# Adjacency in 64x64x64 products, weighted sums set by set in fp32, opening and last step in another order

## The chip, the cores and the metric

The kernel runs on one core of a Trainium2 chip. The metric is the device time of the whole program in microseconds (us), lower is better.

## The reference, cut to what matters

`x` is 128 sets of 64 nodes with 256 features, `adj` a 64x64 matrix of zeros and ones that all sets share.

```python
h = relu(layernorm(x))
q, k, v = h @ Wq.T, h @ Wk.T, h @ Wv.T
rel = adj.T * (q @ k.T)                       # per set, 64 x 64
rel = rel / norm(rel, axis=2)
x = x + rel @ v
h = relu(layernorm(x))
for _ in range(3):                            # gated graph steps
    a = adj @ h                               # in_mat and out_mat are both adj
    av = concat([a, a])
    z = sigmoid(av @ W3.T + b3 + h @ U3.T + bu3)
    r = sigmoid(av @ W4.T + b4 + h @ U3.T + bu3)
    hv = tanh(av @ W5.T + b5 + (r * h) @ U5.T + bu5)
    h = (1 - z) * h + z * hv
out = x + h
```

All of it is fp32. Nothing joins one set with another.

## The kernel before, in words

The 8192 tokens (set and node) are cut into 16 groups of 512 tokens, that is of four pairs of sets: 128 tokens (two sets) fill the 128 partitions, `Q = 4` such pairs stand side by side (`q`). The 256 features are two halves of 128 (`c`, or `o` for outputs). Features stand on the partitions in most products, so that a gate's output is a 128x512 tile in one PSUM bank.

Large products are made in three parts (`product`, L408): each fp32 operand is split into a rounded part `_hi` and a rest `_lo` of type fp32r, and hi*hi, hi*lo and lo*hi are added in PSUM. ScalarE (ACT) makes `_hi` (L724), VectorE (DVE) subtracts to get `_lo` (L921). Small products are plain fp32: the scores (`scores_by_set`, L497), the turns through the identity, and the adjacency product (`adjacency`, L564). A plain fp32 matmul leaves two records in the profile, a fp32r one leaves one.

**Windows.** Two groups, X and Y, run through the three gated steps in turn. One step of one group is a window `w = 6i + k`; even `k` is one group, odd `k` the other. On TensorE (PE) a window is: reset gate from the state (`reset_gate_h`, 12 products into `gate`), reset gate from the adjacency result (`reset_gate_a`, 12), candidate from `a` (12 into `cand`), update gate (12), candidate from `r*h` (12), and then the adjacency product for the next window of the other group into `fea`. That one takes the other group's state as tokens by features (`t_s`, or `h0` at a group's first step) as the stationary operand and multiplies `adjT` with it. `adjT` is 128x128 with `adj.T` twice on its diagonal and zeros elsewhere; so one 128x128x128 product serves two sets, with half of its work on zeros, and a window has 8 of them (4 pairs, 2 feature halves).

Meanwhile DVE updates the other group's state, turns it in blocks of 32, SyncE (SP) sends it to DRAM and back (`turn_state`) to finish the turn, and ACT copies it into `t_s` (`take_back`). After the adjacency product ACT rounds `fea` into `a_hi` and DVE subtracts `a_lo` (`split_a`), which free `fea`.

**Attention beside it.** In the 7 rounds of the loop (6 windows each) windows `k = 2` and `k = 4` also make queries, values and scores of the next groups: `values` writes `tok`, ACT and DVE split it into `v_hi` and `v_lo`; scores go to `fea`, DVE masks them into `S`, ACT rounds `S_hi` and squares `sq`, DVE makes `S_lo`. At the start of windows 3 and 5 `weighted_sum` makes rel @ v from them with 12 fp32r matmuls of 128x128x256. The normalised input `hx` of a group is turned through DRAM as well (`turn_hx`: one store of 512 KB, then four loads).

**Opening and end.** The first two groups pass through an opening that is written out instruction by instruction (weights are split there too, and the product M of Wq and Wk is made in one piece). The last window's state (`new_half`, `transpose_state`) is turned by PE, added to the residual and stored in one piece.

Order is fixed by the code: each engine works its own queue off in program order and waits on semaphores for the others.

## Time and profile before

| | |
|---|---|
| median of 3 runs | 908.33 us (907.57 to 908.65) |
| the profiled execution | 907.36 us, of which 905.6 us is the span of the trace |
| PE busy | 891.7 us, 98% |
| DVE busy | 756.7 us, 84% |
| ACT busy | 520.9 us, 58% |
| granted clock | 0.995 of full over the span |

The time outside the span (1.8 us) is start and end of the program. Busy time of PE is the union of its records; records of successive matmuls overlap, so the distance from one start to the next, and not the length of a record, tells what one costs.

### The profile page before, as it was taken

Reading aid. Unit: us, or ns where it says so; the run is one execution under the profiler, and the core shown is the slowest. Engines: PE = TensorE matmul, PEld = TensorE weight load, DVE = VectorE, ACT = ScalarE, POOL = GpSimd, SP = SyncE. Lnnn points to the kernel's source line nnn. Section 1 sums busy time; section 2 is a strip of 40 time slices with the busy share of each in tenths; the row PEclk is TensorE's granted clock in tenths of the full one; section 3 lists DMA queues with packets and bytes.
Section 4 is the critical chain, followed back from the end, with each engine's and each line's share of the span. In section 5 each row is a group of like instructions: output and inputs, shape, how many; then the busy total and the mean of one; then the engine's idle time right before and its main releaser. Section 6 shows DMA issues by size and latency. Waiting matters only on the chain.

```text
span 905.6 us, 15070 instructions
## 1 busy us (share of the span) xinstructions
PE 891.7 (98%) x4984; PEld 763.0 (84%) x4984; DVE 756.7 (84%) x1527; ACT 520.9 (58%) x892; POOL 111.0 (12%) x161
## 2 busy tenths in 40 slices
PE   8999999999999999999999999999999999999996
PEld 7878888888888888888888888888888888888885
DVE  6888879888799888988988888988879888798665
ACT  5465664656456564665645656556664656555552
POOL 2110102101021010210101101120101101020000
PEclk9999999999999999999999999999999999999998
DMA  6023222623235142441414513154221622233212
GB/s 182 6 69 114 93 94 99 203 69 113 90 123 184 46 142 89 140 167 42 150 58 141 184 69 116 46 176 148 93 93 70 203 98 93 93 116 117 87 54 93
DMA packets 75394, 98.73 MB, mean 109 GB/s; under 512 B 8176, under 2 KB 65776, under 8 KB 75376
## 3 DMA queue, kind: packets, MB, share of 16 engines
q1 hardware_dynamic: 75376, 98.50, 33.0%
q8 instruction: 10, 0.16, 0.1%
q14 instruction: 8, 0.07, 0.0%
HBM read 50.76 MB, written 47.71 MB: 109 GB/s over the span
## 4 chain that ended last, share of the span: by engine, by line
PE 95%; DVE 2%; issue 1%; DMA 1%; ACT 1%; SPq 0%; DVEq 0%
PE gate L410 14%; PE gate L411 14%; PE gate L412 14%; PE cand L410 10%; PE cand L412 9%; PE cand L411 9%; PE fea L564 9%; PE tok L410 3%; PE tok L411 2%; PE tok L412 2%; PE fea L497 2%; PE fea L411 1%; PE fea L410 1%; PE fea L412 1%; DMA x_s<-x 1%
## 5 line engine op out<-in xcount | busy, mean ns | idle before, releaser
L808 ACT ACTIVATE r_s<-gate,b_r 128x512 f32<-128x512 f32 x96 | 65.7, 690 | 123.8 <-PE gate L412 123.8
L1129 DVE TENSOR_TENSOR rh<-r_s,h 128x512 f32<-128x512 f32 x96 | 69.8, 760 | 29.5 <-ACT r_s L808 28.9
L821 ACT ACTIVATE z_s<-gate,b_z 128x512 f32<-128x512 f32 x96 | 64.1, 683 | 48.0 <-PE gate L412 48.0
L827 ACT ACTIVATE c_s<-cand,b_c 128x512 f32<-128x512 f32 x96 | 64.4, 686 | 26.2 <-PE cand L412 25.5
L724 ACT ACTIVATE h_hi<-h 128x512 fp32r<-128x512 f32 x92 | 56.8, 628 | 38.1 <-DVE h L921 22.4
L355 POOL TENSOR_TENSOR rstd<-vare,minus_half 128x4 f32<-128x4 f32 x32 | 42.0, 1312 | 297.3 <-DVE vare L955 297.3
L410 PE MATMUL gate<-h_hi,W_hi_u 128*128 128x512 f32 x192 | 77.9, 406 | 0.2 <-DVE h_lo L921 0.2
L1101 DVE SCALAR_TENSOR_TENSOR d_s<-z_s,h 128x512 f32<-128x512 f32 x96 | 63.5, 685 | 17.5 <-ACT z_s L821 17.5
L410 PE MATMUL cand<-rh_hi,W_hi_u 128*128 128x512 f32 x192 | 76.5, 398 | 0.0
L410 PE MATMUL gate<-a_hi,W_hi_w 128*128 128x512 f32 x192 | 75.0, 390 | 1.1 <-DVE a_lo L921 1.1
L411 PE MATMUL gate<-h_lo,W_hi_u 128*128 128x512 f32 x192 | 75.1, 391 | 0.0
L412 PE MATMUL gate<-h_hi,W_lo_u 128*128 128x512 f32 x192 | 74.8, 390 | 0.0
L412 PE MATMUL cand<-rh_hi,W_lo_u 128*128 128x512 f32 x192 | 74.8, 390 | 0.0
L412 PE MATMUL gate<-a_hi,W_lo_w 128*128 128x512 f32 x192 | 74.8, 390 | 0.0
L411 PE MATMUL gate<-a_lo,W_hi_w 128*128 128x512 f32 x192 | 74.8, 390 | 0.0
L411 PE MATMUL cand<-rh_lo,W_hi_u 128*128 128x512 f32 x192 | 74.8, 389 | 0.0
L412 PE MATMUL gate<-a_hi,W_lo_wz 128*128 128x512 f32 x192 | 74.7, 389 | 0.0
L410 PE MATMUL gate<-a_hi,W_hi_wz 128*128 128x512 f32 x192 | 74.7, 389 | 0.0
L411 PE MATMUL gate<-a_lo,W_hi_wz 128*128 128x512 f32 x192 | 74.7, 389 | 0.0
L410 PE MATMUL cand<-a_hi,W_hi_w 128*128 128x512 f32 x192 | 74.7, 389 | 0.0
L411 PE MATMUL cand<-a_lo,W_hi_w 128*128 128x512 f32 x192 | 74.7, 389 | 0.0
L412 PE MATMUL cand<-a_hi,W_lo_w 128*128 128x512 f32 x192 | 74.7, 389 | 0.0
(150 smaller groups left out, 2202.7 us busy)
## 6 DMA issues: line engine op xcount, KB each, us to landing
h_back<-h_trip SPq DMA_DIRECT2D x216, 128.0 KB, 2.8
h_trip<-h_turned SPq DMA_DIRECT2D x40, 512.0 KB, 2.6
out<-o_s SPq DMA_DIRECT2D x16, 512.0 KB, 3.8
x_s<-x SPq DMA_DIRECT2D x15, 512.0 KB, 4.9
hx_trip<-hx SPq DMA_DIRECT2D x14, 512.0 KB, 3.5
hx_back<-hx_trip SPq DMA_DIRECT2D x56, 128.0 KB, 2.8
h_trip<-h_blk SPq DMA_DIRECT2D x14, 512.0 KB, 3.0
h_trip_last<-h_turned SPq DMA_DIRECT2D x7, 512.0 KB, 3.5
```

The costliest lines, as they stand in the source:

```text
L355: nc.gpsimd.tensor_tensor(rstd[n][:], vare[n][:], minus_half[:], ALU.pow).then_inc(rstd_ready[n], 1)
L410: nc.tensor.matmul(dst, l_hi, r_hi, start=start, stop=False, skip_group_check=True)
L411: nc.tensor.matmul(dst, l_hi, r_lo, start=False, stop=False, skip_group_check=True)
L412: return nc.tensor.matmul(dst, l_lo, r_hi, start=False, stop=stop, skip_group_check=True)
L497: last = nc.tensor.matmul(feaS[half(e), q, half(e)], hxT[:, c, nodes], q_s[:, c, nodes], start=c == 0, stop=c == C - 1)
L564: last = nc.tensor.matmul(fea[:, c, graph_pair(q)], src[:, q, c * P:(c + 1) * P], adjT[:], start=True, stop=True)
L724: return nc.scalar.activation(dst, src, ACT.Copy)
L808: nc.scalar.activation(r_s[:, c, :], gate[:, c, :], ACT.Sigmoid, bias=b_r[:, c:c + 1]).then_inc(r_ready, 1)
L821: nc.scalar.activation(z_s[:, c, :], gate[:, c, :], ACT.Sigmoid, bias=b_z[:, c:c + 1]).then_inc(z_ready, 1)
L827: nc.scalar.activation(c_s[:, c, :], cand[:, c, :], ACT.Tanh, bias=b_c[:, c:c + 1]).then_inc(c_ready, 1)
L1101: nc.vector.scalar_tensor_tensor(d_s[:, c, :], z_s[:, c, :], 1.0, h[s][:, c, :], ALU.subtract, ALU.mult).then_inc(diff_ready, 1)
L1129: nc.vector.tensor_tensor(rh[:, c, :], r_s[:, c, :], h[s][:, c, :], ALU.mult).then_inc(rh_ready, 1)
```

## The change: what it does

1. **Adjacency.** The 8 fp32 products of 128x128x128 of a window become 32 of 64x64x64, one for each set, feature half and half of that (`f`). Each uses a quarter of the array: rows by set (`e`), columns by `f`; the results of set 0 of every pair go to one PSUM bank, those of set 1 to the other. Both banks are now reported full at the end. `split_a` goes by bank (set) in place of feature half, and `reset_gate_a` first makes its 8 matmuls with `a_hi`, then waits for both `a_lo` and makes 4.
2. **Weighted sum** in the loop: 8 fp32 matmuls of 64x64x256 from plain `S` and `v_s` in place of the 12 in fp32r. `v_s` is a plain copy by DVE, so ACT's `v_hi` and `S_hi` and DVE's `S_lo` are gone in the loop. To spread the row halves, two of the four pairs have their sets swapped: `turn_hx` stores in three transfers in place of one, and `square_S` is four instructions of ACT in place of two.
3. A semaphore add on PE (`sources_seen`) that carries the wait stands ahead of these small products, so that none of them is started before its source is there.
4. **Loop.** The two reset gate steps of window 1 stand at the end of the loop body of the round before, not at the start of their own.
5. **Opening**: M is made and split in two halves, group 1's turn goes ahead of the norms of group 0, splits and copies are put in another order on DVE and ACT, norms of group 1 use `fea`. The plain copies of `h` come behind the splits.
6. **Last step** by halves of 256 tokens: candidate, tanh, update, turn and store.

```diff
+        def key_half(q, e):
+            return half(e if q < HQ else 1 - e)
+        def set_columns(t, e):
+            return t[:].rearrange("p c (q e n) -> p c q e n", q=Q, e=2)[:, :, :, e, :]
+        def set_bank(e):
+            return fea[:, e, :].rearrange("p (c q n) -> p c q n", c=C, q=Q)
...
             def turn_hx(g, s):
                 sp.wait_ge(hx_ready, Q * (g + 1))
-                sp.dma_start(hx_trip[s], hx[:].rearrange("p q d -> p (q d)")).then_inc(hx_out, 16)
-                sp.wait_ge(hx_out, 16 * (g - 1))
+                trip, hx_r = rows_by_set(hx_trip[s]), rows_by_set(hx[:].rearrange("p q d -> p (q d)"))
+                sp.dma_start(trip[:, :, 0, :], hx_r[:, :, 0, :]).then_inc(hx_out, 16)
+                for e in range(2):
+                    sp.dma_start(trip[half(1 - e), :, 1, :], hx_r[half(e), :, 1, :]).then_inc(hx_out, 16)
+                sp.wait_ge(hx_out, 48 * (g - 1))
                 blocks_back(hx_back, hx_trip[s], hx_in)
...
-            def weighted_sum(g, n_tok, n_v):
-                pe.wait_ge(S_hi_ready, g + 1)
-                pe.wait_ge(S_lo_ready, g + 1)
-                pe.wait_ge(v_hi_ready, 2 * g + 2)
+            def weighted_sum(n_v, n_rel):
                 tok_done(n_v)
-                for b in range(2):
-                    tok_wait(n_tok, b)
-                    for q in range(HQ * b, HQ * b + HQ):
-                        last = product(tok[:, q, :], (S_hi[:, q, :], S_lo[:, q, :]),
-                                       (v_hi[:, q, :], v_lo[:, q, :]), True, True)
-                    last.then_inc(tok_full, 1)
+                pe.wait_ge(fea_taken, 2 * n_rel + 2)
+                pe.sem_inc(sources_seen, 1)
+                for j in range(HQ):
+                    for q in (j, j + HQ):
+                        for e in range(2):
+                            keys = key_half(q, e)
+                            last = nc.tensor.matmul(tok[half(e), q, :], S[keys, q, keys], v_s[keys, q, :],
+                                                    start=True, stop=True)
+                last.then_inc(tok_full, 2)
...
-            def adjacency(c, src, n):
-                fea_wait(n, c)
-                for q in range(Q):
-                    last = nc.tensor.matmul(fea[:, c, graph_pair(q)], src[:, q, c * P:(c + 1) * P], adjT[:],
-                                            start=True, stop=True)
-                last.then_inc(fea_full, 1)
+            def adjacency(src, n, t_full=None):
+                fea_wait(n, 1)
+                for c in range(C):
+                    if t_full is not None:
+                        pe.wait_ge(t_ready, t_full + c)
+                    if c == 0 or t_full is not None:
+                        pe.sem_inc(sources_seen, 1)
+                    for q in range(Q):
+                        for f in range(2):
+                            part = slice(c * P + f * N, c * P + (f + 1) * N)
+                            for e in range(2):
+                                last = nc.tensor.matmul(set_bank(e)[half(f), c, q, :], src[half(e), q, part],
+                                                        adjT[half(e), half(e)], start=True, stop=True)
+                last.then_inc(fea_full, 2)
...
             def reset_gate_a(w, s, n_a):
-                for c in range(C):
-                    pe.wait_ge(a_hi_ready, 2 * w + (c + 1))
-                    pe.wait_ge(fea_taken, 2 * n_a + (c + 1))
-                    for o in range(C):
-                        last = product(gate[:, o, :], weight("w4", c, o), (a_hi[s][:, c, :], a_lo[s][:, c, :]),
-                                       False, c == C - 1)
-                        if c == C - 1:
-                            last.then_inc(r_full, 1)
+                pe.wait_ge(a_hi_ready, 2 * w + 2)
+                for o in range(C):
+                    for c in range(C):
+                        w_hi, w_lo = weight("w4", c, o)
+                        one(gate[:, o, :], w_hi, a_hi[s][:, c, :])
+                        one(gate[:, o, :], w_lo, a_hi[s][:, c, :])
+                pe.wait_ge(fea_taken, 2 * n_a + 2)
+                for o in range(C):
+                    for c in range(C):
+                        last = one(gate[:, o, :], weight("w4", c, o)[0], a_lo[s][:, c, :], stop=c == C - 1)
+                    last.then_inc(r_full, 1)
...
+            def candidate_rh_last():
+                pe.wait_ge(rh_hi_ready, 2 * LAST)
+                pe.wait_ge(rh_lo_ready, 2 * LAST)
+                for e in range(2):
+                    for o in range(C):
+                        if e == 1:
+                            pe.wait_ge(c_ready, 2 * LAST - 1 + o)
+                        for c in range(C):
+                            last = product(cand[:, o, tokens(e)], weight("u5", c, o),
+                                           (rh_hi[:, c, tokens(e)], rh_lo[:, c, tokens(e)]), False, c == C - 1)
+                        last.then_inc(c_full, 1)
...
             values(0, n("v 0"), (1,))
+            transpose_hx(1, cand, turned_full)
             norms_start(0, n("norm 0"))
-            transpose_hx(1, cand, turned_full)
...
-            def split_a(s, c, n):
-                fea_wait(n, c)
-                copy(a_hi[s][:, c, :], fea[:, c, :]).then_inc(a_hi_ready, 1)
+            def split_a(s, e, n):
+                fea_wait(n, e)
+                copy(set_columns(a_hi[s], e), set_bank(e)).then_inc(a_hi_ready, 1)
...
                 if attention and k == 2:
-                    split_v(use("v X"))
-                    round_S(use("rel X"))
                     square_S(use("rel X"))
...
-            split_weight(3, "w4", sum4)
+            split_weight(3, "u3", raw["u3"])
+            split_weight(4, "w4", sum4)
+            split_S(0)
             take_norm_start(n("norm 0"))
-            split_S(0)
...
-            take_norm(1)
             split_S(1)
-            split_weight(4, "w5", sum5)
+            split_weight(5, "w5", sum5)
+            take_norm_start(n("norm 1"))
+            copy_new_start(0, cand)
...
-            new_half(6 * PAIRS, 1, 0)
-            new_half(6 * PAIRS, 1, 1)
+            for e in range(2):
+                for c in range(C):
+                    new_last(e, c)
             add_resid(G - 1, 1, use_in_end("final 0"), PAIRS - 1)
```

How the rows stand on PE at the end of window 2, where the adjacency product and the weighted sum meet, before (`t_s` the turned state, `v_hi`/`v_lo` and `S_hi`/`S_lo` the split values and scores):

```order
L412 MATMUL cand<-rh_hi,W_lo_u 128x512
L666 REGISTER_ALU
L435 ISA [waits t_ready]
L564 MATMUL fea<-adjT,t_s 128x128 [waits fea_taken]
L564 MATMUL fea<-adjT,t_s 128x128 x3
L666 REGISTER_ALU
L564 MATMUL fea<-adjT,t_s 128x128 [waits fea_taken,t_ready]
L564 MATMUL fea<-adjT,t_s 128x128 x3
L538 REGISTER_ALU
L430 REGISTER_ALU [waits v_hi_ready,S_lo_ready,S_hi_ready]
```

The same place of PE in the changed kernel (`S` and `v_s` are the plain scores and values):

```order
L436 MATMUL cand<-rh_hi,W_lo_u 128x512
L462 ISA
L587 REGISTER_ALU [waits fea_taken]
L594 MATMUL fea<-adjT,t_s 64x64 [waits t_ready]
L594 MATMUL fea<-adjT,t_s 64x64 x15
L587 REGISTER_ALU
L594 MATMUL fea<-adjT,t_s 64x64 [waits t_ready]
L594 MATMUL fea<-adjT,t_s 64x64 x15
L457 REGISTER_ALU
L562 REGISTER_ALU [waits tok_taken]
L568 MATMUL tok<-v_s,S 64x256 [waits fea_taken]
L568 MATMUL tok<-v_s,S 64x256 x7
```

Eight products became 32, and the twelve matmuls of the weighted sum behind them became eight that use quarters of the array too; the waits for `S_hi`, `S_lo` and `v_hi` are gone.

On DVE the end of the attention's work in window 2 (`v` the values in `tok`, `S` the masked scores, `sq` their squares), before:

```order
L921 TENSOR_TENSOR v_lo<-tok,v_hi 128x512
L927 ISA
L1000 TENSOR_TENSOR S<-fea,mask 64x4x64 x2
L921 TENSOR_TENSOR S_lo<-S,S_hi 128x512
L1025 STREAM_TRANSPOSE sq_turned<-sq 128x256
L1028 TENSOR_REDUCE sq_part<-sq_turned 128x8
```

And in the changed kernel:

```order
L1072 COPY v_s<-tok 128x512
L1002 ISA
L1081 TENSOR_TENSOR S<-fea,mask 64x4x64 x2
L1106 STREAM_TRANSPOSE sq_turned<-sq 128x256
L1109 TENSOR_REDUCE sq_part<-sq_turned 128x8
```

`S_lo` is gone from DVE's row, and the subtraction that made `v_lo` is a copy that waits for PE alone.

## Rows read from the trace of the kernel before

**Rows 1.** The page, part 1: busy us (share of the span) and instructions.
```profile
PE 891.7 (98%) x4984; PEld 763.0 (84%) x4984; DVE 756.7 (84%) x1527; ACT 520.9 (58%) x892; POOL 111.0 (12%) x161
```
**Rows 2.** Stretches from adjacency to adjacency: us; PE, PEld, DVE, ACT, POOL busy; PEclk.
```profile
164.92:180.32 15.40, 15.40 (x77) 13.05 (x76) 13.45 (x30) 10.37 (x18) 2.73 (x3) 1.00 0.53 179
180.32:202.62 22.30, 22.30 (x145) 19.25 (x144) 18.90 (x38) 11.74 (x22) 1.01 (x1) 1.00 0.22 73
...
241.78:258.63 16.85, 16.85 (x90) 14.49 (x89) 16.31 (x40) 7.92 (x13) 2.43 (x2) 1.00 0.18 62
...
sum 109.11, PE 109.11 PEld 93.50 DVE 94.25 ACT 64.15 POOL 14.19; mean PE 18.18 PEld 15.58 DVE 15.71 ACT 10.69 POOL 2.36
```
**Rows 3.** Waits of PE: who for whom, us in total, times, longest.
```profile
PE tok L557 <- DVE h L921: 2.7, 1, 2.7
PE tok L410 <- issue: 2.1, 2, 1.5
PE gate L410 <- DVE a_lo L921: 1.1, 1, 1.1
```
**Rows 4.** Groups of PE by shape: adjacency and scores; busy us, mean ns.
```profile
L564 PE MATMUL fea<-adjT,t_s 128*128 128x128 f32 x512 | 62.2, 275 | 0.0
L564 PE MATMUL fea<-adjT,h 128*128 128x128 f32 x256 | 31.2, 275 | 0.1
L497 PE MATMUL fea<-q_s,hxT 128*64 128x64 f32 x448 | 16.1, 225 | 0.0
```
**Rows 5.** Timeline of PE, an adjacency product: start, length, what.
```profile
865.94 1.95 PE L564 MATMUL fea<-adjT,t_s 128*128 128x128 f32 x16
867.64 0.48 PE L410 MATMUL gate<-h_hi,W_hi_u 128*128 128x512 f32 x1
867.95 0.40 PE L411 MATMUL gate<-h_lo,W_hi_u 128*128 128x512 f32 x1
```
**Rows 6.** Timeline of PE, one group's scores and their neighbours.
```profile
128.52 0.28 PE L412 MATMUL tok<-W_hi_v,hxT_lo 128*128 128x256 f32 x1
128.73 1.15 PE L497 MATMUL fea<-q_s,hxT 128*64 128x64 f32 x32
130.15 0.39 PE L411 MATMUL cand<-rh_lo,W_hi_u 128*128 128x512 f32 x1
```
**Rows 7.** Timeline of PE cut at 128.745 (scores) and at 865.98 (adjacency).
```profile
128.73 0.28 PE L497 MATMUL fea<-q_s,hxT 128*64 128x64 f32 x2
...
865.94 0.27 PE L564 MATMUL fea<-adjT,t_s 128*128 128x128 f32 x1
```
**Rows 8.** Timeline of PE in the opening: the product M, 128x256 in fp32.
```profile
7.40 1.89 PE L676 MATMUL gate<-d_s 128*128 128x256 f32 x8
```
**Rows 9.** Timelines of ACT and DVE: last `a_hi` and `a_lo` of window 1's adjacency.
```profile
182.30 0.60 ACT L724 ACTIVATE a_hi<-fea 128x512 fp32r<-128x512 f32 x1 [0.30 <-PE fea L564]
...
185.09 0.65 DVE L921 TENSOR_TENSOR a_lo<-fea,a_hi 128x512 fp32r<-128x512 f32 x1
```
**Rows 10.** Timelines of SP and DVE: the turn of group X's `hx`.
```profile
177.62 0.34 SPq L242 DMA_DIRECT2D hx_trip<-hx  x1
181.38 1.75 SPq L237 DMA_DIRECT2D hx_back<-hx_trip  x4
...
185.67 1.28 DVE L969 STREAM_TRANSPOSE hxT<-hx_back 128x512 f32<-128x512 f32 x2
```
**Rows 11.** Timelines of PE and DVE in the opening.
```profile
41.06 0.36 PE L410 MATMUL tok<-v_hi,S_hi 128*128 128x256 f32 x1 [1.53 <-issue]
...
40.27 0.69 DVE L921 TENSOR_TENSOR S_lo<-S,S_hi 128x512 fp32r<-128x512 f32 x1
```
**Rows 12.** Timelines of DVE and SP at the end.
```profile
895.55 1.29 DVE L1092 TENSOR_TENSOR o_s<-h_back,resid 128x512 f32<-128x512 f32 x2
898.80 0.69 DVE L921 TENSOR_TENSOR h<-c_s,d_s 128x512 f32<-128x512 f32 x1
...
902.17 0.40 SPq L338 DMA_DIRECT2D out<-o_s  x1
```

230 lines of the change are left out of this document (140 added, 90 removed).

## The prediction, made before the changed kernel had run

> **What bounds the kernel now.** I read the page's busy times first. PE is busy for 98% of the span, the next engine, DVE, for 84% [rows 1]. An average can hide a stage with another limit, so the stretches of a round come next: window by window, from one adjacency product to the next, PE is busy for exactly as long as the stretch lasts, and the sum over a round's six windows is 109.11 us of 109.11 [rows 2]. The table of PE's waits has only single waits, all in the opening and at the end [rows 3]. So in the loop each microsecond taken from PE's row is a microsecond of the kernel, as long as the others keep up, and each one added is lost. DVE is the one to watch: 94.25 us in a round of 109.11, and 16.31 of 16.85 in window 5 [rows 2].
>
> A record's length says little on PE, because records overlap; I use distances between starts.
>
> **The adjacency product.** A window's product is 16 records (8 matmuls, two records each) and there are 512 + 256 records [rows 4], so 48 windows have one. It begins at 865.94; the two records behind it start at 867.64 and 867.95, and a fp32r matmul of 512 columns takes 0.227 us: a window without attention has 60 of them and this product in 15.40 us [rows 2], (15.40 - 1.78) / 60. So it ends at 867.95 - 0.23 = 867.72 and costs 1.78 us, 0.112 per record of 128 columns [rows 5]. Half of its multiplications are with the zeros of `adjT`.
>
> The new one has 64 records of 64 columns, each on a quarter of the array. No row shows quarters; the nearest is the scores: 32 records of 64 columns, each on half of the array's columns. The values in front end at 128.52 + 0.12 = 128.64 (0.12 for 256 columns, below), the candidate behind starts its second matmul at 130.15, so the scores take until 129.92: 1.28 us with getting in and out [rows 6]. Their 1.15 us less the 0.22 of a last record's own length leave 0.93, 0.058 for two records. How do two records fit into 0.058, when one of 128 columns takes 0.112? Cut at 128.745 the timeline has two records of the scores, started within 15 ns, while on the whole array only one is there 40 ns after the start [rows 7]. So two products on different column halves run side by side, and the hardware even takes the second half's product past the second record of the first (the records of one product must follow each other, as on the whole array). I take it that row halves do the same: four records for each 0.058 us, 16 such steps, and so the time of the scores, 1.28 us. That saves 1.78 - 1.28 = 0.50 us in each of 48 windows: **24.0 us**. Bounds from the nearest rows: nothing better than four at a time with no price for entry and exit, 0.93 us, -40.8 us in all; and, with one product for each 0.058 us, 32 steps and the same 0.35 us of entry and exit, 2.21 us, +20.6 us in all. I take the value in between, because the scores' row is the nearest in shape and kind and its price for a change of mode is in it.
>
> Here the Trainium skill speaks against the change: "PSUM — Partial Sum Buffer", section on engine and sequencer instructions, says that matmuls start and complete in program order. By that rule the second record of a product holds up the next product on another quarter; the scores' rate would come out the same (one product a step), and the adjacency would take the 2.21 us. The two starts within 15 ns [rows 7] do not look like that order, since the first product's own second record can't be one of them. It stays a rival.
>
> **The weighted sum.** Windows that begin with it last 16.85 us, those without anything extra 15.40 [rows 2]: 1.45 us for 12 matmuls of 256 columns, 0.12 each. It becomes 16 records of 256 columns on quarters, directly behind the adjacency, so with no other change of mode. A record of 256 columns in fp32 on the whole array takes (1.89 - 0.38) / 7 = 0.216 us, 0.38 being the last one's length [rows 8]. Four steps of it are 0.87 us. 14 x (1.45 - 0.87) = **8.1 us**. The bound from above, one product a step and a step for the last one's second record, is 9 x 0.216 = 1.94 us, +6.9 us in all. From below 0.87 stands: a quarter can't take its columns faster than the whole array does. I take 0.87, with the adjacency's reading.
>
> **What the other engines do meanwhile.** The loop's windows become 0.5 us shorter, those with a weighted sum 1.1. Is anybody late then?
> - `a_hi` used to be rounded for the first feature half while the second was still multiplied; now both banks come at the end. Last `a_hi` ended 182.90, counted from the product's start at 180.32 2.6 us [rows 2, 9]. Now the banks are there at 1.3 + 0.2, two rounds of 0.6 follow: 2.8. `reset_gate_a` starts at 1.28 + 12 x 0.227 = 4.0. Cover: 1.2 us; cost none.
> - `a_lo` ended at 185.74, 5.4 us after the product's start [rows 9], in an order of DVE that stays. It is now wanted at 4.0 + 8 x 0.227 = 5.8. Cover 0.4 us, none lost; in the opening's last window, where PE waited 1.1 us for it [rows 3], the new order gives that back.
> - DVE in window 5 had 16.31 us of work, 0.7 of it `S_lo`, which goes; the window becomes 15.8. It can run behind by 0 to 0.3 us and catch up in the next, which has 2 us to spare. Over a round DVE has 94.25 - 1.4 = 92.9 us to do in 109.1 - 4.1 = 105.0. Cost none; if it were not caught up, 7 x 0.3 = 2 us.
> - `turn_hx` issues three stores at 0.34 us each where there was one, in pieces of half a KB; issue to the loads' issue was 3.8 us, and the loads' end falls about where DVE turns it, at 185.67 [rows 10]. I expect it 1 to 2 us later. Queued behind it on DVE is `rh` of window 2, which then is late too; but the candidate that wants it has queries, values and scores before it, 6.9 us (22.30 - 15.40 [rows 2]). Cost none. SP's next state transfer is behind these stores by under 1 us, with the same cover.
> - The waits moved onto semaphore adds stand on PE's sequencer; before it lie 12 matmuls, 2.7 us, with waits long over. `tok` by a plain copy costs DVE what the subtraction did. Moving `reset_gate` of window 1 past the loop's end changes no instruction, and no wait of PE stands there now [rows 3]. Cost none.
>
> **Opening.** PE waits 1.5 us before the second weighted sum at 41.06 [rows 3, 11]; its DVE row is `S_lo` at 40.27 [rows 11], behind the norms that wait for PE. In the new order `S_lo` comes before the norms, and the two copies of `h` (2 x 0.6) are moved behind it. I count 1.5 us. The wait for `a_lo` is 1.1. The halves of M, and the turn that now fills the wait for the squares, I put at 0.9 us together, within 0 (something else is late then) and 2. Sum **3.5 us**, 1 to 5.
>
> **End.** The candidate by halves costs 24 matmuls of 256 columns where there were 12 of 512: 24 x 0.12 - 12 x 0.227 = +0.16 us. DVE is the limit: it finishes the other group's output until 896.84, then 4 operations until 899.49 [rows 12]; now it has 8 of about 0.4, until 900.0. Then half of the turn, half of the addition: the last store is issued at about 901.7 in place of 902.17 [rows 12] and is half as large. **0.8 us**, from 2 gained to 0.5 lost.
>
> **Sum** against the profiled execution's own 907.36 us (905.6 span, 1.8 around it): 24.0 + 8.1 + 3.5 + 0.8 = 36.4, so 871.0. The median stands 1.0 above that execution: **872 us**. Own range 865 to 881, from 0.1 us of entry and exit more or less per window (5 us), opening and end.
>
> **Rivals.**
> 1. *Products in order (slower).* One step a product: +20.6 and +6.9, less 4.3 of opening and end: +23.2, 931 us. It decides when two records of one product cannot be passed by another quarter's; it turns the sign once a window's product takes over 1.78 us. For it: the rate of the scores alone, which both readings explain. Against it: the two starts [rows 7].
> 2. *PE can't start records faster (slower, or nearly the same).* The closest starts on average are 0.93 / 32 = 29 ns [rows 6]. If that is the issue and not the columns, 64 records take 1.86 + 0.35 = 2.21 us (+20.6), while the weighted sum's long records still gain 8.1: +20.6 - 8.1 - 4.3 = +8.2, 916 us. Against it: two starts within 15 ns. The Trainium skill ("TensorE: Matmul & The Clock Gate", section "Wait — 56ns, not 53.3ns?") gives a floor of about 25 ns between two starts, however few the columns; no row here shows it, and by it 64 records would take 1.6 us and the whole come to an estimated 904.
> 3. *A new wait.* Shorter windows meet a chain that doesn't shrink: state turned, stored, loaded, `t_s`; or the late `hx`. At 0.3 us in each of 48 windows, 14.4 us of the gain are lost: 886 us; at worst all of the loop's 32.1, and 904 is left. For it: DVE's 16.31 of 16.85; against it: the covers above.
>
> **Chances.** Forecast 0.70; rival 1 0.10; rival 2 0.06; rival 3 0.14. The range reaches from the forecast's lower end to the worst of rival 3: 864 to 906, with under 0.2 outside, most of it rivals 1 and 2. Under 0.2% (1.8 us) this kernel's measurement tells nothing. Faster: the forecast and rival 3 less 0.01, 0.83; slower: rivals 1 and 2 less 0.01, 0.15; those two hundredths are the chance of the same.
>
> **What would show it.** In the new profile 64 records of an adjacency product within 1.15 us, the window without attention at 14.9 us from product to product and the one with a weighted sum at 15.8, four starts within some 30 ns, then a gap of 58; ACT's and DVE's waits for PE shorter, no wait of PE for `a_hi`, `a_lo` or `t_s`. If the records come in twos, the window lasts 15.8 and rival 1 or 2 holds (1: the weighted sum takes 1.9 us too; 2: it takes 0.9). If the product takes 1.3 us and the window is still over 15.1, PE has a new wait with a name, and rival 3 holds. I am wrong in the main point if quarters don't run four at a time.

## The result and the profile after

The changed kernel takes 917.69 us (median of 4 runs, 916.27 to 919.55) where the kernel before takes 908.33: a ratio of 1.0099, 95% interval 1.0086 to 1.0112. It is slower by 1%; the forecast was 872 us. The profiled execution took 917.08 us, 915.3 of them in the trace.

From the page of the changed kernel: part 1 (busy us, share, instructions), the granted clock in 40 slices, and the queue that brings instructions (pieces, MB, share).

```profile
PE 881.5 (96%) x7356; PEld 718.7 (79%) x7356; DVE 750.6 (82%) x1518; ACT 493.4 (54%) x881; POOL 122.3 (13%) x161
...
PEclk9999999899998999989999899999999999999998
...
q8 instruction: 72, 1.18, 0.5%
```

The last two lines on the page of the kernel before:

```profile
PEclk9999999999999999999999999999999999999998
...
q8 instruction: 10, 0.16, 0.1%
```

PE's share fell from 98% [rows 1] to 96%, some slices in the middle show less than the full clock, and 1.18 MB of instructions were fetched where 0.16 were. Now the round window by window, as in [rows 2] (us; PE, PEld, DVE, ACT, POOL busy; PEclk, DMA share, GB/s):

```profile
160.41:181.83 21.42, 18.00 (x126) 14.04 (x125) 14.00 (x31) 10.49 (x19) 2.72 (x3) 0.84 0.51 162
181.83:203.65 21.82, 21.82 (x194) 18.41 (x193) 18.17 (x38) 10.56 (x20) 1.01 (x1) 1.00 0.14 50
203.65:219.57 15.92, 15.92 (x142) 12.79 (x141) 14.20 (x36) 10.44 (x19) 1.80 (x2) 1.00 0.39 118
219.57:241.91 22.34, 22.11 (x194) 18.33 (x193) 17.56 (x30) 12.52 (x24) 3.05 (x6) 1.00 0.32 106
241.91:257.80 15.89, 15.89 (x141) 12.78 (x141) 15.38 (x37) 7.32 (x13) 2.43 (x2) 1.00 0.20 67
257.80:272.81 15.01, 15.01 (x126) 12.14 (x125) 13.72 (x22) 8.90 (x16) 4.98 (x7) 1.00 0.63 197
sum 112.40, PE 108.75 PEld 88.49 DVE 93.03 ACT 60.23 POOL 16.00; mean PE 18.12 PEld 14.75 DVE 15.51 ACT 10.04 POOL 2.67
```

Four windows are shorter, as forecast or nearly, and the fourth row's is as long as before (22.34). The first row, the answer to 15.40 us [rows 2], lasts 21.42. It is the one in which PE's loop jumps back. There are six such windows: 21.42, 21.48, 21.70, 21.67, 19.98 and 20.34 us. PE's waits name the same place six times, and the second row is new too (who for whom, us in total, times, longest); before there was one wait for `a_lo`, in the opening [rows 3]:

```profile
PE cand L434 <- issue: 19.8, 6, 3.4
PE gate L439 <- DVE a_lo L996: 2.5, 8, 0.9
```

"Issue" says that PE waited for no other engine: nothing was handed to it by its sequencer, the unit that reads PE's instructions in order, takes the waits and the jumps, and hands the products on. PE's timeline there (start, length, what, idle time ahead):

```profile
165.94 0.39 PE L439 MATMUL gate<-a_hi,W_lo_w 128*128 128x512 f32 x1
166.17 1.09 PE L439 MATMUL gate<-a_lo,W_hi_w 128*128 128x512 f32 x4
170.69 0.79 PE L434 MATMUL cand<-a_hi,W_hi_w 128*128 128x512 f32 x1 [3.42 <-issue]
171.28 0.63 PE L435 MATMUL cand<-a_lo,W_hi_w 128*128 128x512 f32 x1
171.70 0.63 PE L436 MATMUL cand<-a_hi,W_lo_w 128*128 128x512 f32 x1
172.13 0.63 PE L434 MATMUL cand<-a_hi,W_hi_w 128*128 128x512 f32 x1
```

The last products of the body end at 167.26, the first of the next pass starts 3.42 us later, and from there starts are 0.427 us apart instead of 0.227: the granted clock is at the lower of its two levels, 1.2 in place of 2.4 GHz. The trace's records of the jumps and of the stretches at the lower clock say it for all six (us):

```
                          before            changed kernel
jump taken, six times     0.234 0.213 0.208 4.33  4.08  4.17  4.31  4.04  4.33
                          0.208 0.207 0.208
lower clock in the loop   none              6.8   6.8   6.8   6.8   3.4   3.4
```

The six windows are 36.6 us longer than six of 15.0. PE idles for 19.8 us of that. Of the 34.0 us at the lower clock 3.5 lie in the idle time (in the first window it falls at 169.73, before the product at 170.69), and half of the other 30.6, 15.3 us, is lost by products at half the rate. That leaves 1.5 us. About 1.0 of it is that the idle time is counted from the end of the last record, 0.16 us behind the place where the next product would have started (0.39 - 0.227).

The product itself did what was forecast (PE's timeline, the whole product, and the same cut at 181.845):

```profile
181.83 1.16 PE L594 MATMUL fea<-adjT,t_s 64*64 64x64 f32 x64
182.92 0.50 PE L434 MATMUL gate<-h_hi,W_hi_u 128*128 128x512 f32 x1
...
181.83 0.28 PE L594 MATMUL fea<-adjT,t_s 64*64 64x64 f32 x3
```

64 records in 1.16 us, three of them begun within 15 ns [rows 7 for before]. In PE's compiled code the two matmuls of a product stand one behind the other, both on the same quarter of the array. The plain window fell from 15.40 to 14.92 us behind the loop.

### The profile page after: what moved, and what is told of

It is laid out like the page before. It is cut to its first block, busy times and chain, and to the rows that moved or that the text cites. A ratio compares the mean times of both kernels' runs of the same rounds, so it can differ in the third digit from the quotient of the medians.

```text
span 915.3 us, 19786 instructions
## 1 busy us (share of the span) xinstructions
PE 881.5 (96%) x7356; PEld 718.7 (79%) x7356; DVE 750.6 (82%) x1518; ACT 493.4 (54%) x881; POOL 122.3 (13%) x161
## 3 DMA queue, kind: packets, MB, share of 16 engines
q8 instruction: 72, 1.18, 0.5%
## 4 chain that ended last, share of the span: by engine, by line
PE 69%; issue 14%; DVE 10%; ACT 3%; POOL 3%; DMA 1%; DVEq 0%; SPq 0%; POOLq 0%; ACTq 0%
PE gate L439 10%; PE cand L434 8%; PE gate L434 8%; PE cand L435 7%; PE cand L436 7%; PE gate L435 7%; PE gate L436 7%; PE fea L594 4%; DVE c_s L1190 2%; PE fea L524 2%; POOL rstd L379 2%; PE tok L434 2%; PE tok L435 1%; PE tok L436 1%; PE fea L434 1%
## 5 line engine op out<-in xcount | busy, mean ns | idle before, releaser
L870 ACT ACTIVATE r_s<-gate,b_r 128x512 f32<-128x512 f32 x96 | 60.8, 685 | 106.0 <-PE gate L439 106.0
L434 PE MATMUL cand<-a_hi,W_hi_w 128*128 128x512 f32 x192 | 80.5, 419 | 19.8 <-issue 19.8
L1222 DVE TENSOR_TENSOR rh<-r_s,h 128x512 f32<-128x512 f32 x96 | 66.4, 732 | 18.7 <-ACT r_s L870 17.5
L434 PE MATMUL gate<-h_hi,W_hi_u 128*128 128x512 f32 x192 | 80.3, 418 | 0.3 <-DVE h_lo L996 0.3
L436 PE MATMUL cand<-a_hi,W_lo_w 128*128 128x512 f32 x192 | 79.8, 416 | 0.0
L435 PE MATMUL cand<-a_lo,W_hi_w 128*128 128x512 f32 x192 | 79.8, 415 | 0.0
L776 ACT ACTIVATE rh_hi<-rh 128x512 fp32r<-128x512 f32 x96 | 58.2, 631 | 38.8 <-DVE rh L1222 38.8
L434 PE MATMUL cand<-rh_hi,W_hi_u 128*128 128x512 f32 (+1 forms) x196 | 77.3, 394 | 0.0
L436 PE MATMUL cand<-rh_hi,W_lo_u 128*128 128x512 f32 (+1 forms) x196 | 75.5, 385 | 0.0
L435 PE MATMUL cand<-rh_lo,W_hi_u 128*128 128x512 f32 (+1 forms) x196 | 75.4, 385 | 0.0
```

Source lines behind the costliest of these rows:

```text
L434: nc.tensor.matmul(dst, l_hi, r_hi, start=start, stop=False, skip_group_check=True)
L435: nc.tensor.matmul(dst, l_hi, r_lo, start=False, stop=False, skip_group_check=True)
L436: return nc.tensor.matmul(dst, l_lo, r_hi, start=False, stop=stop, skip_group_check=True)
L776: return nc.scalar.activation(dst, src, ACT.Copy)
L870: nc.scalar.activation(r_s[:, c, :], gate[:, c, :], ACT.Sigmoid, bias=b_r[:, c:c + 1]).then_inc(r_ready, 1)
L1222: nc.vector.tensor_tensor(rh[:, c, :], r_s[:, c, :], h[s][:, c, :], ALU.mult).then_inc(rh_ready, 1)
```

## The experiments

I held three theories on the long windows. **A:** the loop body of PE has grown from 1316 to 1908 instructions (each small product is a weight load and a matmul, twice in fp32), and is too long to be still at hand when the loop jumps back. **B:** the step moved to the body's end, or the small products themselves, make the wait. **C:** the clock falls because the small products are too light. Theory **E** came with the first run: part of what is missing besides is PE waiting for the second `a_lo`. All runs are compared with runs of the kernel before made beside them on the same chip (908.4 to 909.6 us). The counts of instructions are those of PE's compiled code, numbered from its beginning. The instruction queue's row counts pieces: 1.18 MB in 72 are 16 KB each, which is 256 instructions (2732 instructions of the kernel before are 10.7 such pieces, and 10 were fetched).

### 1 and 2. No jump

```diff
-            with pe.Fori(0, PAIRS - 1) as i:
+            for i in range(PAIRS - 1):
```

On PE alone, in the changed kernel and in the kernel before. The loop has seven rounds and so six jumps back; the expectations' "six times" are these jumps.

> TensorE's loop of the changed kernel is written out six times and every other engine keeps its loop, so TensorE's work and every wait are the same and only the jump back at the end of a round is gone. Theory A (the changed loop body of 1908 TensorE instructions is too long to be still at hand when the jump goes back to its first one; the jump took 4.33 us, the instruction queue moved 1.18 MB against 0.16, and the windows that begin with the jump took 21.42, 21.48, 21.70, 21.67, 19.98 and 20.34 us against 15.0 for their like): these windows fall to 15.0, 36.9 us go, 878 to 881 us. Theory B (the window is long because of the work moved to the body's end and the products' order, not because of the jump): the time stays at 912 to 919. Theory C (a clock that falls because the small products are too light): no change at the window, and half clock there as before.

> The same edit in the kernel before: TensorE's loop written out six times. Theory A: its body of 1316 instructions is still at hand at the jump (0.234 us for the jump in the trace), so nothing is to be had: 906 to 909 us. If writing the loop out helps every such kernel (a rival to A: the jump always costs), it falls by more than 3 us. If straight code is fetched too slowly to keep up, it is longer.

Measured: changed kernel 883.9 us, ratio 0.9716 (0.9700 to 0.9732); kernel before 909.4, ratio 1.0003 (0.9993 to 1.0014). So the jump costs the changed kernel 34 us and the kernel before nothing. Theory B would have left the order and the products in place, and with them the loss; it is out, and so is "a loop always costs". Theory C is out too: with the same small products the loop of this run has no stretch at the lower clock. 883.9 is 3 to 6 above what I expected, and 12 above the forecast. Windows of the changed kernel without its jump, and PE's wait for `a_lo` over the whole execution:

```profile
161.14:176.28 15.14, 15.14 (x126) 12.09 (x125) 13.79 (x30) 9.70 (x19) 2.72 (x3) 1.00 0.53 171
176.28:198.56 22.28, 22.12 (x194) 18.33 (x193) 18.29 (x38) 11.10 (x22) 1.01 (x1) 1.00 0.29 93
198.56:214.34 15.78, 15.78 (x142) 12.63 (x141) 14.06 (x36) 10.45 (x19) 1.67 (x2) 1.00 0.39 119
214.34:236.82 22.48, 22.11 (x193) 18.33 (x192) 17.70 (x30) 12.63 (x24) 3.21 (x6) 1.00 0.31 105
```

```profile
PE gate L439 <- DVE a_lo L996: 4.6, 14, 0.9
```

With the stall gone the two windows with queries are 22.28 and 22.48, for a forecast of 21.8. DVE's timeline around the second tells why (start, length, what, idle time ahead), and below it PE's:

```profile
213.51 1.29 DVE L1185 SCALAR_TENSOR_TENSOR d_s<-z_s,h 128x512 f32<-128x512 f32 x2
215.10 0.17 DVE L1034 SCALAR_TENSOR_TENSOR shift<-mv,rstd 128x4 f32<-128x4 f32 x1 [0.30 <-POOL rstd L379]
215.22 0.69 DVE L1190 TENSOR_TENSOR c_s<-z_s,c_s 128x512 f32<-128x512 f32 x1
...
219.92 0.65 DVE L996 TENSOR_TENSOR a_lo<-fea,a_hi 128x512 fp32r<-128x512 f32 x1
```

```profile
220.63 1.19 PE L439 MATMUL gate<-a_lo,W_hi_w 128*128 128x512 f32 x4 [0.37 <-DVE a_lo L996]
```

From the first `c_s` of an update to the end of the second `a_lo` DVE has eight operations in a row, 5.35 us in this window as in the others that I read, before and after. Here they begin 0.88 us after the adjacency product's start (214.34), because statistics and `shift` of the next group are ahead of them; before it was 0.19. So `a_lo` ends at 6.2 us and PE wants it at 5.8. In the other window the row starts 0.68 us after it instead of 0.07: ACT, with one `hx` more ahead, makes the tanh later.

### 3 and 4. The jump in the kernel before, and the moved step

```diff
+            round_of(0)
-            with pe.Fori(0, PAIRS - 1) as i:
+            with pe.Fori(0, (PAIRS - 2) // 2) as j:
+                round_of(2 * j + 1)
+                round_of(2 * j + 2)
```

> The kernel before, its first round of TensorE written out ahead of the loop and two rounds in each body: 2628 instructions in a body, two jumps back in place of six, the products and waits all as in the kernel before. Theory A: each of the two jumps costs what it costs in the changed kernel (5.0 to 6.7 us), 918 to 922 us, and two windows of over 20 us stand in the trace. Theory B (the cause is in the changed order or the small products): no window is long, 906 to 909.

Measured: 914.2 us, ratio 1.0048 (1.0032 to 1.0064). The jumps are there, 3.60 and 3.96 us, and 44 pieces of instructions were fetched where the code has 21, but their windows are 17.4 and 17.9 us and not over 20. PE's wait at the first (its place in the code: the start of a body) and the window:

```profile
385.20:402.64 17.44, 15.71 (x77) 13.13 (x77) 14.26 (x31) 10.93 (x19) 2.18 (x3) 1.00 0.50 168
```

```profile
PE gate L410 <- ACT h_hi L729: 1.7, 1, 1.7
```

The sequencer reaches the jump nearly 2 us before the last matmuls are done, so 1.7 us of 3.6 are seen, and after so short a gap the clock stayed up. The row names `h_hi`, which had long been there: a wait that follows a stall of the sequencer takes its name. So theory A's stall is there in the kernel before, and its price was set too high.

```diff
             with pe.Fori(0, PAIRS - 1) as i:
+                first_reset_gate(i)
...
-                first_reset_gate(i + 1)
+            first_reset_gate(PAIRS - 1)
```

> The changed kernel with the reset gates of window 1 back at the loop body's top, where the kernel before has them; body of 1905 instructions instead of 1908. Theory A: the stall stays, 914 to 920 us. Theory B (moving them behind the loop body's end put a wait at the jump): the long windows are gone, 878 to 885.

Measured: 913.4 us, ratio 1.0035 (1.0017 to 1.0052), windows at the jump 19.77 to 21.61, jumps of 3.3 to 3.7 us. The stall doesn't depend on the moved step. The six windows add up to 3.4 us less than in the changed kernel. Most of that is the lower clock: outside the idle time there are 25.0 us of it in place of 30.6, worth 2.8. What makes a jump last 3.3 or 4.3 us stays open.

### 5 and 6. Length alone

`filler` is a semaphore that nobody waits for; 592 or 300 adds stand in the loop body of the kernel before, five or three in each three-part product, ahead of its third matmul, until they are used up.

```diff
+                for _ in range(min(5, left[0])):
+                    pe.sem_inc(filler, 1)
+                    left[0] -= 1
                 return nc.tensor.matmul(dst, l_lo, r_hi, start=False, stop=stop, skip_group_check=True)
```

> The kernel before, with 592 semaphore adds put between TensorE's matmuls of its loop body and nothing else: the body has the changed kernel's 1908 instructions and the products, waits and tiles of the kernel before. TensorE's sequencer is ahead of its matmuls, so an add by itself should cost nothing. Theory A (a body of this length is not at hand at the jump): six jumps that take 3.3 to 4.3 us each, as in the changed kernel, windows behind them 2 to 6.5 us longer, 920 to 947 us, and the instruction queue moves over 1 MB. Theory D (the stall needs the quarters' records or the changed order): 906 to 912 and jumps of 0.2 us.

> The same with 300 adds: a body of 1616 instructions, between the 1316 that jump in 0.21 us and the 1905 that don't. Theory A leaves open on which side it lies: either no stall (906 to 910 us, jumps 0.2 us) or the full one. A stall that grew with the length would show here a jump of about half the price, 1.8 to 2.2 us.

Measured: 592 adds 1038.4 us (ratio 1.1427, 1.1408 to 1.1446), 300 adds 909.8 (1.0017, 1.0005 to 1.0030). I was wrong on the price of an add: five in a row hold the next matmul up (14.4 us in a round's windows 2 to 5), three don't. But the jump can be read beside it: 3.59 to 3.73 us and 72 pieces with 592, 0.22 us and 11 pieces with 300. So the body's length alone brings the stall, with the products of the kernel before, and it does not grow with the length: it is there or not.

### 7 and 11. `a_lo` before the turn

```diff
                 split_a(w, s, 0)
+                if both:
+                    split_a(w, s, 1)
                 turn_half(w, o, 1)
-                split_a(w, s, 1)
+                if not both:
+                    split_a(w, s, 1)
```

With the straight loop; `both` in every window, and then in windows 2 and 4 alone.

> TensorE's loop written out and, on VectorE, both `a_lo` ahead of the second turn of the state instead of one on each side of it. In the run with the straight loop the windows that should have been 15.4 - 0.5 = 14.9 lasted 15.0 to 15.15 and those with queries 22.29 and 22.47 for an expected 21.8: TensorE waits for the second `a_lo`, 4.6 us in 14 single rows of over 0.3 us and 11 us by the windows. Theory E (these waits are the rest of what my forecast missed): the second `a_lo` is done 0.6 us earlier, windows of 14.9, 15.8 and 21.8, 872 to 876 us. Rival: VectorE has no time to spare, its turn of the state comes 0.6 us later and the wait moves to `t_s` or `h_lo`: 880 to 886.

> TensorE's loop written out, and both `a_lo` ahead of the second turn of the state in windows 2 and 4 alone, where TensorE waited longest for it and the turned state is wanted over 8 us later. Against the run that did so in all windows (880.1 us; its windows 1 and 0 got no shorter or longer, with VectorE's `h` waiting for its transfer), the turn is late nowhere that counts. Theory E: windows 2 and 4 at 21.8 to 21.95 instead of 22.29 and 22.47, the others as in the first run, 8 x 1.0 us: 875 to 878 us. Rival (VectorE itself is full there): 880 to 884.

Measured: in every window 880.1 us (877.5 to 881.1; ratio 0.9676, 0.9658 to 0.9694), in two windows **877.8** (0.9648, 0.9632 to 0.9664). Both sides of the first expectation were partly right. The windows with queries fell to 21.82 and 21.93 in three rounds of seven, but in others they grew to 23.05 and 22.75, and windows 1 to between 15.2 and 16.3 in six rounds (14.9 to 15.6 without the edit). There DVE waits for its state to come back, 1.5 us, where without the edit it waited 0.4. The first row is of the run with `both` everywhere, the second of the straight loop without it:

```profile
DVE h L1044 <- DMA h_back<-h_trip: 1.5, 1, 1.5
```

```profile
DVE h L1044 <- DMA h_back<-h_trip: 0.4, 1, 0.4
```

In two windows alone, a round is what the forecast's first two terms make of it, but for the last row:

```profile
176.94:198.76 21.82, 21.82 (x194) 18.41 (x193) 18.30 (x38) 11.55 (x22) 1.01 (x1) 1.00 0.31 95
198.76:214.54 15.78, 15.78 (x142) 12.63 (x141) 14.06 (x36) 10.45 (x19) 1.67 (x2) 1.00 0.39 121
214.54:236.41 21.87, 21.87 (x194) 18.33 (x193) 17.77 (x30) 12.66 (x24) 3.21 (x6) 1.00 0.32 107
236.41:252.19 15.78, 15.78 (x142) 12.63 (x141) 15.28 (x37) 7.32 (x13) 2.43 (x2) 1.00 0.20 68
252.19:267.29 15.10, 15.10 (x125) 12.13 (x124) 13.96 (x22) 9.04 (x16) 4.99 (x7) 1.00 0.62 192
```

### 8. Quarters in half of the windows, loop kept

`adjacency_whole` is the adjacency of before; windows 3, 5 and 0 use it.

```diff
+                    (adjacency_whole if k in (3, 5, 0) and in_loop else adjacency)(...)
```

> The changed kernel with its loop, but three of the loop's six adjacency products as in the kernel before, on the whole array with 128x128 (the windows 3, 5 and 0; with them the order of their banks by features): the body has 1617 instructions instead of 1908. Each such window gives back 0.48 us of what the change gained, 7 x 3 x 0.48 = 10 us. Theory A with no stall at this length: 917 - 37 + 10 = 888 to 895 us, jumps of 0.2 us. With the stall still there: 924 to 930.

Measured: 886.3 us, ratio 0.9754 (0.9737 to 0.9770), jumps of 0.21 us, 14 pieces. With half of the loop's quarters' products the kernel is 31 us faster than with all of them. The expected 888 to 895 was 2 us too high at its lower end.

### 9 and 12. Row halves

```diff
-                        for f in range(2):
-                            part = slice(c * P + f * N, c * P + (f + 1) * N)
-                            for e in range(2):
-                                last = nc.tensor.matmul(set_bank(e)[half(f), c, q, :], src[half(e), q, part],
-                                                        adjT[half(e), half(e)], start=True, stop=True)
+                        for e in range(2):
+                            last = nc.tensor.matmul(set_bank(e)[:, c, q, :], src[half(e), q, c * P:(c + 1) * P],
+                                                    adjT[half(e), half(e)], start=True, stop=True)
```

> The changed kernel with its loop, but the adjacency by row halves alone: 32 records of 64 columns in place of 64, each with 128x64 (all feature columns, half of the rows), two sets side by side. The loop body falls from 1908 to about 1524 instructions, so no stall at the jump. If the columns streamed through set the pace (two records in 0.058 us, 16 steps), the product takes 1.28 us as with quarters: 880 to 886 us. If loading the 128 weight columns sets it (0.107 us a step, the pace of the whole-array product in the kernel before), it takes 16 x 0.107 + 0.35 = 2.06 us, window 15.7: 912 to 922 us.

> The loop kept, row halves for the adjacency, and `a_lo` early in windows 2 and 4: a version that might be best. If row halves run at the pace of the columns: 873 to 879 us. If the weight loads set the pace, 912 to 922 and `a_lo` doesn't matter.

Measured: 915.2 us (ratio 1.0064, 1.0047 to 1.0081) and 915.8 (1.0069, 1.0052 to 1.0085); jumps of 0.21 us. The product and its window in the first of them:

```profile
180.48 2.00 PE L592 MATMUL fea<-adjT,t_s 64*128 64x64 f32 x32
182.41 0.50 PE L434 MATMUL gate<-h_hi,W_hi_u 128*128 128x512 f32 x1
```

```profile
164.72:180.48 15.76, 15.76 (x94) 13.05 (x93) 13.82 (x30) 10.32 (x19) 2.72 (x3) 1.00 0.54 170
```

15.76 less the 13.62 of a window's other products (15.40 - 1.78) is 2.14 us for the product: (2.14 - 0.35) / 16 = 0.112 us a step, although only 64 columns stream through. Two records start at a time, within 7 ns, and the next two 0.105 us later, so the row halves do run side by side. The step is that of the whole-array product [rows 5], which streams 128. Both load 128 weight columns, where the scores and the quarters load 64 and take 0.058 us a step [rows 6]. So in these four products it is the number of weight columns that goes with the pace, and not the number streamed. No wait for `a_lo` is left, so moving it brings nothing.

### 10. The adjacency's term by itself

The straight loop, and `adjacency_whole` in all 42 windows of the loop.

> TensorE's loop written out as in the first run, and the loop's 42 adjacency products as in the kernel before (128x128 on the whole array, banks by features): what is left of the change is the weighted sum, the opening, the end and 6 quarters' products outside the loop. My term for the product: 42 x 0.50 = 21 us are given back, 883.9 + 21 = 905. Theory E (part of that gain was lost in waits for the second `a_lo`, which this kernel doesn't have): only 42 x 0.48 - 11 = 9 us are given back, 891 to 895 us, windows of 15.4, 16.3 and 22.3.

Measured: 899.9 us, ratio 0.9897 (0.9881 to 0.9914). Between my two numbers: 16 us are given back against the straight loop, and 22 against the run with `a_lo` early in two windows. Neither is the product alone, for the weighted sum costs more here as well. Its window:

```profile
200.87:217.51 16.64, 16.64 (x93) 13.64 (x92) 14.62 (x37) 10.75 (x19) 2.38 (x2) 1.00 0.40 124
```

16.64 - 15.40 = 1.24 us for the same weighted sum that costs 15.78 - 14.92 = 0.86 behind a product on quarters: 0.38 us is the price of one more change of mode (between the whole array and parts of it), which I had put at 0.35 from the scores. So 42 products at 0.48 are 20.2 us, and 14 changes of mode 5.3. Windows 0 and 1 of the quarters' kernels are too long by 3 us in all (up to 15.6 for 14.92), which leaves 22.5, against 22 measured; the straight loop without the early `a_lo` loses some 7 more in windows 2 and 4, which leaves 16. The product is worth 20 us of the 21 forecast for it.

### 13 and 14. Length or pieces

Both: loop kept, quarters in windows 2 to 5, `a_lo` early in 2 and 4, body of 1714 instructions. In the second, 152 adds are spread over PE's opening (four in a product, `left = [152]`), so that the body begins at instruction 1033 and not 881. In pieces of 256 instructions it is 4 to 10 instead of 3 to 10.

> The changed kernel with its loop, the adjacency of windows 0 and 1 on the whole array as before, and both `a_lo` early in windows 2 and 4: a body of 1714 instructions that begins at TensorE's instruction 881. The instruction queue moves pieces of 16 KB, 256 instructions; this body touches 8 such pieces, as the two that stalled did (1908 from 881; 1908 from 633), while the ones that didn't stall touch 6 or 7. If what counts is the number of pieces: six slow jumps, 905 to 920 us. If it is the plain length, with a limit somewhere between 1617 and 1905: either, and its shifted twin the same as this one.

> The same kernel with 152 semaphore adds spread over TensorE's opening, so that the same body of 1714 instructions begins at 1033 and touches 7 pieces. Counting pieces: jumps of 0.2 us and 880 to 885 us (the best of the straight ones, 877.8, plus 7 x 2 x 0.4 for the two products on the whole array), where its twin stalls. Counting length: as its twin.

Measured: 913.4 us (908.5 to 914.8; ratio 1.0055, 1.0038 to 1.0072) and **885.0** (0.9735, 0.9719 to 0.9751). The profiled execution of the first is its fastest: its mean granted clock is 0.992, that of the other three 0.982 to 0.985. The instruction queue, the window at the jump and PE's wait of the one over eight pieces:

```profile
q8 instruction: 68, 1.11, 0.5%
```

```profile
160.79:180.68 19.89, 17.31 (x78) 14.11 (x77) 13.92 (x31) 10.64 (x19) 2.72 (x3) 0.91 0.53 167
```

```profile
PE cand L437 <- issue: 17.4, 6, 3.1
```

The queue and the window of the one over seven:

```profile
q8 instruction: 15, 0.25, 0.1%
```

```profile
163.19:178.59 15.40, 15.40 (x78) 13.05 (x77) 13.83 (x30) 10.09 (x19) 2.73 (x3) 1.00 0.54 175
```

The same body, shifted by 152 instructions, is 28 us faster. Length alone would have left the two alike. Nor is it how far on the body ends: that of run 14 ends at 2746, behind those of runs 5 and 13 (2540 and 2594). That what counts is the number of pieces touched is read from the table, where all kernels with a loop line up (run 3 takes two jumps, the others six; run 12 is as run 9):

```
body      from   pieces   jump, us       pieces fetched   run
1316       633   6        0.21           10               before
1524       753   7        0.21           12               9
1616       633   7        0.22           11               6
1617       881   7        0.21           14               8
1714      1033   7        0.21 to 0.24   15               14
1714       881   8        4.0 to 4.4     68               13
1908       633   8        3.6 to 3.7     72               5
1906       831   8        3.3 to 3.7     69               4
1908       881   8        4.0 to 4.3     72               changed kernel
2628      1908   11       3.6 to 4.0     44               3
```

## Why the prediction was wrong, step by step

- **"I am wrong in the main point if quarters don't run four at a time."** They do, and the prediction is wrong all the same. What was missing is a term: nowhere did I count what the change does to the length of PE's loop. The profile had the queue of instructions and its 0.16 MB, and the diff makes 32 products out of 8. The sentence that stood in its place was **"Moving `reset_gate` of window 1 past the loop's end changes no instruction, and no wait of PE stands there now [rows 3]. Cost none."** I looked at the loop's edge and asked only which waits move over it, not what the jump itself would cost. It costs 36.6 us: 19.8 idle, 15.3 by products at the lower clock, 1.5 around them. Shown by runs 1, 5, 13 and 14. The Trainium skill, "Runtime: NRT & Kernel Launch", section "Instruction fetch mechanics", says that PE holds 2048 instructions, refilled in blocks of 256, and that a taken branch out of its current two-page window must fetch the target first. The blocks agree with runs 13 and 14. The window here is wider than two pages, since bodies over seven jump in 0.21 us; and a body of 1714 instructions, fewer than 2048, still stalls when it lies over eight.
- **Adjacency, 24.0 us.** 0.50 us a window was forecast, 0.48 measured (15.40 to 14.92). Right, on the scores' pace and their price of entry. Rivals 1 and 2 are out: the product takes 1.30 us (1.78 - 0.48) and not 2.21, and of three records begun within 15 ns two would have to be on one quarter if the order of the code held. The Trainium skill, "PSUM — Partial Sum Buffer", section "Engine vs sequencer instructions", says that matmuls start and complete in program order. The trace doesn't agree for matmuls on different quarters.
- **Weighted sum, 8.1 us.** 0.87 us each was forecast; 0.86 with the straight loop, 0.98 (15.90 - 14.92) in the loop of the changed kernel, 1.7 us more in all. The timelines of PE, first the changed kernel and then the straight loop, show where 0.10 of the 0.12 arise:

```profile
203.65 1.16 PE L594 MATMUL fea<-adjT,t_s 64*64 64x64 f32 x64
204.68 1.09 PE L568 MATMUL tok<-v_s,S 64*64 64x256 f32 x16
205.70 0.50 PE L434 MATMUL gate<-h_hi,W_hi_u 128*128 128x512 f32 x1
```

```profile
198.56 1.16 PE L594 MATMUL fea<-adjT,t_s 64*64 64x64 f32 x64
199.54 1.05 PE L568 MATMUL tok<-v_s,S 64*64 64x256 f32 x16
200.51 0.50 PE L434 MATMUL gate<-h_hi,W_hi_u 128*128 128x512 f32 x1
```

  Counted from the adjacency's start, the weighted sum begins at 1.03 us in the loop and at 0.98 without it, and what follows at 2.05 and 1.95, much the same in all 14. In the loop PE's sequencer works the wait's number out in registers first, and the add `sources_seen` ends at 0.97; in straight code the wait's number is fixed and the add ends at 0.78. I had said of the adds that 12 matmuls lie before them; before this one only the adjacency does. That the late add is the cause is argued from the times, no run takes it away alone.
- **"Cover 0.4 us, none lost" (`a_lo`)** failed, and with it "It can run behind by 0 to 0.3 us and catch up in the next". I measured the cover from the product's start, as if DVE's order were tied to it. It is tied to what stands ahead on DVE and ACT, and that did not get shorter with PE. DVE ran 0.7 us late in window 4, and a late `a_lo` is felt at once. In the changed kernel it costs 0.5 us in window 4 of a round, 22.34 for 21.82, some 3.6 us; PE's stall gave the others time. Without the stall moving it is worth 6.1 us (883.9 to 877.8), which is also why taking the jump away gave 33.8 us and not 36.6. It is rival 3 at about half its price, with the place wrong: that named `t_s` and the late `hx`.
- **Rounded `a_hi` and `turn_hx`:** no wait of PE for either in the loop. Right.
- **Opening, 3.5 us.** The third adjacency product starts at 69.44 instead of 71.18, and 2 x 0.48 of the 1.74 are the product's own. 0.8 is left, and even that can't be put down to the new order. The kernel before ran at the lower clock under products for 3.41 us there, up to 1.7 us lost, and the changed kernel's profiled execution has no such stretch. That is chance:

```profile
22.48:25.89 3.41, 3.41 (x15) 3.22 (x15) 3.41 (x8) 1.98 (x4) 0.51 (x1) 0.50 0.01 2
```

  Run 11, with the changed opening, has one (from 24.18), run 1 has none, and their third products start at 71.23 and 70.18; the four times of run 11 lie two by two, 876.6 and 876.9 against 878.7 and 878.8. So no gain of the new order up to the third product is shown. At the first `gate` from `a_hi` PE was 3.6 us ahead (38.99 for 42.57), by the second adjacency product only 1.1 (53.30 for 54.37). Part of what was lost between went into new waits: `W_lo_wz` 0.6 and the turn of `h` 0.5; `a_lo` still takes 0.9 of 1.1. I had counted what goes and not what is late next.
- **End, 0.8 us.** From the last product's start to the end 22.63 us for 24.24, 0.48 of it the product: 1.1. Right.

Against the 871.0 of my sum for the profiled execution, 917.1 is 46.1 more: 36.6 from the jump, 3.6 from `a_lo` in window 4, 2.7 from the opening, 1.7 from the weighted sum, 0.9 from the 0.02 in 47 products; the rest is under one microsecond.

The best version is the straight loop with `a_lo` early in two windows, 877.8 us; the best with a loop is run 14, 885.0. For the last 5.8 us to 872, the opening's 2.7 and windows 0 and 1 at 15.1 and 15.0 to 15.6 (3 us in all) account for nearly all.

## What to carry to other kernels

Before an edit that multiplies small instructions inside a hardware loop, count the loop body, and the pieces of 256 it touches, and compare with the instruction queue's row. Where nothing stalled, that row showed as many pieces as the code has (10 to 15 in the kernel before and in runs 6, 8, 9 and 14). In the changed kernel it showed 72 for a code of 15: 9 to 10 more for each jump, the body and a little over. Here a body over seven pieces was free, and one over eight or more cost 3.3 to 4.4 us of the sequencer a jump and, most times, the clock behind it; writing the loop out, shortening it, or shifting its start are three ways out. And a cover is measured from what releases the late engine, not from the event that the fast engine sets.

## What the runs showed of the hardware that I had not expected

- Four fp32 products of 64x64x64 on the quarters of the array proceed together: a step of all four takes 0.058 us, the same as a step of two column halves [rows 6]. Row halves with 128 weight columns take 0.112 a step.
- The price of a refetching jump is 3.3 to 4.4 us of the sequencer. What PE feels is that less the lead of its sequencer: 1.7 to 2.2 us where the adjacency product on the whole array lies ahead of the jump (runs 3 and 5), 2.6 to 3.4 where four matmuls with `a_lo` do (the changed kernel and run 13), and 3.3 to 3.8, all of it, where the product on quarters does (run 4).
- Behind gaps of 3.3 us on average the clock went to 1.2 GHz each of six times in the changed kernel, for 3.4 or 6.8 us, and behind 3.6 in run 4 as well; behind gaps of 2.9 in run 13 four times of six, behind 1.8 in run 5 three times of six, behind 1.7 and 2.2 in run 3 never.
- Semaphore adds on PE are hidden at three to each group of three matmuls (0.2 us a round for 300) and aren't at five.
- Straight code is fetched fast enough: the kernel before with 10,334 PE instructions in place of 2,732 fetched 40 pieces and lost nothing (1.0003).
